# Graph attention on one core: the adjacency cast to bf16 on its way in, by DMAs issued from POOL, two chunks at a time

## The reference

```python
h = jnp.maximum(_layernorm(x, axis=-1), 0.0)          # x: 8 x 2048 x 256 fp32
Wh = jnp.einsum('bnf,fo->bno', h, W)                   # W: 256 x 256
e = (Wh @ a1)[:, :, None] + (Wh @ a2)[:, None, :]
e = jnp.where(e >= 0, e, ALPHA * e)                    # ALPHA = 0.2
attention = jnp.where(adj > 0, e, MASK_FILL)           # adj: 8 x 2048 x 2048 int32
attention = jax.nn.softmax(attention, axis=1)          # over i, the rows
out = x + jax.nn.elu(jnp.einsum('bij,bjo->bio', attention, Wh))
```

## Time and profile before

| | |
|---|---|
| median of 3 runs | 1041.62 us (1041.38 to 1043.15) |
| profiled execution | 1041.01 us |
| its span, first to last instruction | 1039.2 us |
| TensorE busy | 952.9 us, 92% |
| VectorE busy | 962.6 us, 93% |
| ScalarE busy | 937.5 us, 90% |
| POOL busy | 487.7 us, 47% |
| mean granted TensorE clock | 0.994 |
| DMA | 194.82 MB, 323235 packets, 65.6% of 16 engines for the main queue |

### The profile page before, as it was taken

One profiled execution on the slowest core, in us unless ns is written; L12 is line 12 of the kernel. 1 busy time (PEld: TensorE's weight loads), 2 busy tenths in 40 slices (PEclk: granted clock), 3 DMA queues, 4 the chain that ended last, 5 costly groups with the idle time before them and its releaser, 6 DMA issues. The chain is left out here.

```text
span 1039.2 us, 24022 instructions
## 1 busy us (share of the span) xinstructions
PE 952.9 (92%) x8971; PEld 827.7 (80%) x8971; DVE 962.6 (93%) x1259; ACT 937.5 (90%) x1479; POOL 487.7 (47%) x510
## 2 busy tenths in 40 slices
PE   4677999999999999999999999999999999888897
PEld 3565888888888888888888888888888888777786
DVE  5799999999999999999999999999999999999963
ACT  2599999999999999999999999999999999988873
POOL 3344333545445454454545545355454453554543
PEclk9999999999999999999999999999999999999999
DMA  8466565777767677677676767667767666757514
GB/s 233 118 182 185 162 187 162 206 202 203 198 183 208 198 200 212 179 211 201 196 205 178 215 198 204 195 182 207 204 196 208 187 191 175 199 170 200 153 52 152
DMA packets 323235, 194.82 MB, mean 187 GB/s; under 512 B 7472, under 2 KB 319024, under 8 KB 323120
## 3 DMA queue, kind: packets, MB, share of 16 engines
q1 hardware_dynamic: 323120, 193.29, 65.6%
HBM read 176.42 MB, written 16.84 MB: 186 GB/s over the span
## 5 line engine op out<-in xcount | busy, mean ns | idle before, releaser
L418 PE MATMUL acc<-v,direct 128*128 128x256 f16 x1024 | 279.3, 273 | 14.9 <-ACT z_direct L522 7.8
L654 DVE CUSTOM_DVE_ANT_0 prob<-tp,f_row 128x2048 f32<-128x2048 bf16 x128 | 291.8, 2280 | 0.0
L422 PE MATMUL acc<-v,direct 128*128 128x256 f16 x1024 | 279.1, 273 | 0.0
L420 PE MATMUL acc<-v,direct 128*128 128x256 f16 x1024 | 279.1, 273 | 0.0
L401 PE MATMUL acc_st<-v,stored 128*128 128x256 f16 x992 | 270.4, 273 | 0.0
L402 PE MATMUL acc_st<-v,stored 128*128 128x256 f16 x992 | 270.4, 273 | 0.0
L400 PE MATMUL acc_st<-v,stored 128*128 128x256 f16 x992 | 270.4, 273 | 0.0
L743 POOL TENSOR_SCALAR small_total<-total 128x1 f32<-128x1 f32 x128 | 47.7, 373 | 470.4 <-ACT prob L488 470.4
L488 ACT ACTIVATE prob<-prob,shift 128x2048 f32<-128x2048 f32 x128 | 256.5, 2004 | 10.5
L481 ACT ACTIVATE prob<-prob,f 128x2048 f32<-128x2048 f32 x128 | 255.7, 1998 | 0.0
L749 POOL TENSOR_TENSOR direct<-prob,inv 128x1024 f16<-128x1024 f32 x128 | 242.3, 1893 | 10.0
(11 more groups left out here) (81 smaller groups left out, 1263.4 us busy)
## 6 DMA issues: line engine op xcount, KB each, us to landing
raw<-in_adj SPq DMA_DIRECT2D x128, 1024.0 KB, 5.9
y<-in_x SPq DMA_DIRECT2D x64, 256.0 KB, 5.1
out<-y SPq DMA_DIRECT2D x64, 256.0 KB, 3.1
x_in<-in_x SPq DMA_DIRECT2D x108, 128.0 KB, 5.1
f_row<-f_scratch SPq DMA_DIRECT2D x31, 256.0 KB, 5.0
stored<-in_x SPq DMA_DIRECT2D x4, 512.0 KB, 7.8
f_scratch<-f_t SPq DMA_DIRECT2D x124, 0.5 KB
stored<-in_x SPq DMA_DIRECT2D x4, 128.0 KB, 2.2
```

Of the source, the lines that this page charges most:

```text
L418: nc.tensor.matmul(acc[:, m, :], p_d[:, 0, rows], v_c[:, 0, :], start=(j == 0 and m % 2 == 0), stop=False, skip_group_check=True)
L420: nc.tensor.matmul(acc[:, m, :], p_d[:, 0, rows], v_c[:, 1, :], start=False, stop=False, skip_group_check=True)
L422: last = nc.tensor.matmul(acc[:, m, :], p_d[:, 1, rows], v_c[:, 0, :], start=False, stop=(j == C - 1), skip_group_check=True)
L654: nc.vector.tensor_tensor_reduce(out=prob[:, c % 2, :], in0=tp_b, in1=f1_row[:, b % 2, :], scale=1.0, scalar=-3.0e38, op0=ALU.add, op1=ALU ...
```

## The change

The adjacency is brought in as bf16. A DMA that changes the type is issued from POOL, so `load_raw` moves from SP to POOL. It brings two chunks at once: 128 partitions x 16 rows x 256 columns, pieces of 1024 B in memory that become 512 B in `raw`. `raw` keeps two buffers, each now for a pair of chunks in bf16 (the same bytes per buffer as before). Pairs 0 and 1 are issued in steps -17 and -10 ahead of POOL's other work, the others in even steps after the split and the residual addition and before `root`, once the masks of the pair that used the buffer are made. `make_mask` waits on the pair's semaphore and reads its half of the buffer; its operation is the same, with bf16 input in place of int32.

```diff
--- before.py
+++ after.py
@@ -10,7 +10,6 @@
 F32 = mybir.dt.float32
 F16 = mybir.dt.float16
 BF16 = mybir.dt.bfloat16
-I32 = mybir.dt.int32
 
 P = 128
 ALPHA = 0.2
@@ -58,7 +57,7 @@
         def sem(name):
             return ctx.enter_context(nc.semaphore(name))
 
-        raw = sb("raw", [P, 2, C, P], I32)
+        raw = sb("raw", [P, 2, C, 2 * P], BF16)
         neg = sb("neg", [P, 2, C, P], BF16)
         f1_row = sb("f1_row", [P, 2, N], F32)
         prob = sb("prob", [P, 2, N], F32)
@@ -273,11 +272,6 @@
                     sp.wait_ge(xn_ready, c - RX + 1)
                 sp.dma_start(x_buf(c), x[c // C, c % C * P:(c % C + 1) * P, :]).then_inc(x_in_s[(c - EARLY) % RX], 16)
 
-            def load_raw(c):
-                wait(sp, neg_ready, c - 1)
-                sp.dma_start(raw[:, c % 2], adj[c // C].rearrange("(c p) j -> p c j", p=P)[
-                    :, :, c % C * P:(c % C + 1) * P]).then_inc(raw_in[c % 2], 16)
-
             def write_f1(piece):
                 sp.wait_ge(f1_turned, pieces_sent(piece + 1))
                 b, q = divmod(piece, 4)
@@ -303,13 +297,9 @@
                 sp.dma_start(x_early[:, 4 * g:4 * g + 4, :],
                              x[4 * g // C, r:r + 4 * P, :].rearrange("(c p) f -> p c f", p=P)
                              ).then_inc(x_early_in[3 + g], 16)
-            load_raw(0)
-            load_raw(1)
             for c in range(EARLY, EARLY + RX):
                 load_x(c)
             for s in range(FIRST, END + 2):
-                if chunk(s + 3) and s + 3 >= 2:
-                    load_raw(s + 3)
                 if chunk(s + 24) and s + 24 >= EARLY + RX:
                     load_x(s + 24)
                 if chunk(s + LEAD - 1) and (s + LEAD - 1) % 4 == 3 and sent((s + LEAD - 1) // 4):
@@ -637,9 +627,10 @@
                                                op0=ALU.mult, op1=ALU.mult).then_inc(offset_s, 1)
 
             def make_mask(c):
-                dve.wait_ge(raw_in[c % 2], 16 * (c // 2 + 1))
+                pair = c // 2
+                dve.wait_ge(raw_in[pair % 2], 16 * (pair // 2 + 1))
                 wait(dve, tp_ready, c - 1)
-                nc.vector.tensor_scalar(neg[:, c % 2], raw[:, c % 2], 0.0, -NOT_AN_EDGE, ALU.is_le, ALU.mult
+                nc.vector.tensor_scalar(neg[:, c % 2], raw[:, pair % 2, :, c % 2 * P:(c % 2 + 1) * P], 0.0, -NOT_AN_EDGE, ALU.is_le, ALU.mult
                                         ).then_inc(neg_ready, 1)
 
             def mask_scores(c):
@@ -735,6 +726,13 @@
             nc.gpsimd.tensor_copy(ident_b[:], ident[:]).then_inc(ident_ready, 1)
             pool.wait_ge(const_ready, 1)
 
+
+            def load_raw(pair):
+                wait(pool, neg_ready, 2 * pair - 2)
+                b, q = divmod(pair, C // 2)
+                nc.gpsimd.dma_start(raw[:, pair % 2], adj[b].rearrange("(c p) j -> p c j", p=P)[
+                    :, :, 2 * P * q:2 * P * (q + 1)]).then_inc(raw_in[pair % 2], 16)
+
             def split_high(c):
                 p = prob[:, c % 2, :]
                 k = inv[:, c % R:c % R + 1]
@@ -768,10 +766,16 @@
                 nc.gpsimd.tensor_tensor(pair, pair, elu[:, k % RE, :], ALU.add).then_inc(y_ready, 1)
 
             for s in range(FIRST, END + 2):
+                if s == -17:
+                    load_raw(0)
+                if s == -10:
+                    load_raw(1)
                 if chunk(s - 1):
                     split_high(s - 1)
                 for k in finish(s - 2):
                     finish_add(k)
+                if s % 2 == 0 and s >= 0 and chunk(s + 4):
+                    load_raw(s // 2 + 2)
                 if chunk(s + LEAD + 2) and s < 0:
                     normalise(s + LEAD + 2)
                 c = measured_at(s)
```

## The result

The changed kernel takes 1029.26 us (median of 4 runs, 1027.53 to 1030.56); the kernel before, in the same comparison, 1041.84 us (4 runs, 1041.38 to 1043.15). The ratio is 0.9874, 95% interval 0.9861 to 0.9888: 1.3% faster, 12.6 us. Forecast were 1029.0 us. The profiled execution of the changed kernel took 1030.56 us around a span of 1028.8 us, 10.45 us less than that of before.

The account below looks back on a forecast made before the run. VectorE, TensorE and ScalarE, within 2% of each other, form one ring that bounds the kernel. From 1041.0 us, -13.6 - 4.5 + 2 + 3.3 = -12.8 gives 1028.2, as median 1029; own range 1012 to 1037, whole range up to 1085.

Parts of the forecast that it names:

- The mask pass, 0.68 us: VectorE's mask pass: halving the input's bytes halves the time per column again, 1217 ns to 0.68 us, 0.53 us a step.
- What of it reaches the end, 2.0 us a batch: Steps 2 to 110: only what ScalarE gets back of its waits counts, 124.0 in place of 126 us a batch, -13.6 us.
- The steps to show it, 7.75 us: Sign in the steady steps: a step takes 7.75 us, where the profile was read as 7.88.
- The last steps: Last 17 steps, without projection: the mask pass stands once in a ring over two steps, -4.5 us.
- The issue, 2.5 us: POOL's time per new load, taken as 2.5 us between 0.37 and 3.8; in steady steps mostly hidden, +2 us.
- In root steps the root is behind the issue ... VectorE is 0.3 late every fourth step: 0: Steady root steps: root comes 2.2 us later, offsets start 1.85 us after its end; VectorE's 0.53 gain covers it, cost 0.
- Before the first step, +3.3: Start: nothing hides the first two issues among the normalisations; 0.8 us of one and all 2.5 of the other exposed.
- Data and DMA engines, 0: New loads have 16.5 us to land and need 11.8 at the old rate; DMA engines 70% busy: cost 0.
- The issue holds VectorE off: Rival on VectorE: its splits grow past 1.5 us in even steps; chance 0.08.
- POOL becomes the bound: Rival: at an issue of 5 us and more POOL's idle time overflows by 8.4 us a batch, 1089 us; chance 0.22.
- The cast slows the transfer: Rival on the loads: beyond 1.4 times the old time per byte data come late, at 1.6 times about 1160; chance 0.05.
- The pass stays: Rival on the mask pass: it stays at 1.2 us and only the costs are left, 1047 us; chance 0.05.

Follow-up runs that it names:

- the run with the pass alone: The kernel before, its loads unaltered on SP, with the mask pass reading half of each piece as bf16: 1020.62 us, ratio 0.9801.
- the run with the earlier first loads: The changed kernel with `root` ahead of the issue, and the first two loads issued behind the normalisations of steps -19 and -15: 1023.36 us, ratio 0.9833.
- the additions: The changed kernel with `root` ahead of the issue and two small two-input POOL instructions behind each issue from step 0 on: 1049.38 us.

## Why the prediction was right, point by point

- **The mask pass, 0.68 us.** Right: 685 ns, in place of 1217 with four-byte input. Less the 148 ns reckoned as fixed that is 0.26 ns a column, half of 0.52.
- **What of it reaches the end, 2.0 us a batch.** The mechanism was right, the size 16% low: -16.2 us against -13.6 in the run with the pass alone. In the batch from step 64 to 80 ScalarE's idle time falls from 5.3 to 3.2 us there, so the 2.0 were met. The term left out is 0.6 us a batch more, which is not work that went: ScalarE's instructions add up to 133.0 and 132.9 us, but overlap each other by 16.4 us in place of 15.9, as fewer gaps lie between them. The parts of the 2.0 were the wrong way round: it was to be the waits for the projection that go and those for POOL that stay. In that run the projection's stay (1.5 us) and POOL's fall to 0.9. The steps to show it, 7.75 us, came out at 7.48 (814.98 / 109), since they were reckoned from 7.88 in place of 7.64. The last steps: -3.9 and -4.0 against -4.5.
- **The issue, 2.5 us.** No run shows this term. An issue takes 1.25 us (1248 ns, 64 times), half of it, between the price below (0.37) and the lower one above (3.8), nearer to the first.
- **"In root steps the root is behind the issue ... VectorE is 0.3 late every fourth step: 0".** This is the step that failed. It took `root` at its 1.01 us from the earlier trace rows and moved it. Moved behind the issue it starts while VectorE's two-input splits run and takes 1.2 to 2.0, 1.6 on the mean. For three root steps of four the 0 was right all the same. At s = 4 mod 16, where the sum has +0.3 a batch, the addition has pushed it under the second split: VectorE waits 0.93 us for it, and the batch loses 0.84. The route costs 6.3 us in the steady steps where +2 was forecast, in the step that was named, at three times the price; 3.3 of the 6.3 go when `root` stands first. The earlier trace rows has a case of two such instructions side by side, a split of 2.27 us beside an addition of 1.27, where splits with no addition beside them take 1.24 to 1.29; the route's sum holds nothing of the kind for `root`.
- **Before the first step, +3.3.** Measured +3.4 at step 2, of other parts. With the issue at 1.25 us the prediction's own working gives 0 for the first (17.22 is before the 17.71 at which TensorE takes the block) and 1.25 for the second. Of the profiles with these loads in this place and nothing else disturbed, those that keep TensorE's clock have the scores of step 0 at 45.5 us, 1.35 behind the 44.16 with the old loads: the working holds. 1.4 more come in other executions from TensorE's clock (last section), and 1.6 in the profiled one alone, in which the load of the weights landed after 5.1 us (2.9 to 3.5 in the others) and the first normalisation began at 9.32 us (7.1 to 7.7).
- **Data and DMA engines, 0.** Right: no wait of VectorE for a load is listed in the steady stretch, and the issue's wait for the masks is 6.9 us once, early, as the group line shows.

So the total was right in part by luck, since errors cancel: in the steady steps a gain 2.6 us too small and a route cost 4.3 too small, at the start an issue twice too long, which in the executions with a lower clock looks right.

**The rivals.** *The issue holds VectorE off* (chance 0.08), as the addition does with the split in the earlier trace rows (2.27 us): not in the changed kernel. The splits beside issues keep their 1.24 to 1.29 us, and no mask pass lies beside one. Where one does, with `root` first, it goes from 0.68 to 1.38 us (twice), to 1.38 in three steps of the run with the earlier first loads, and to 1.42 in each of six batches with the additions. Once in each of these runs, near 50 us, it was the issue that grew, to 1.62 to 1.63 us, while the pass kept 0.69. So the rival is real for the mask pass and a matter of place: mostly the pass got longer, by 0.70 to 0.74 us, and near 50 us the issue, by 0.4. *POOL becomes the bound:* not at 1.25 us, but nearer than was reckoned. About 4.0 us in place of 1.25 as given make 1091, where the prediction had put the even point at 3.8 us and 1089 only at 5; its count of idle time before the one-column instruction left out that `root` stood behind the issue. 1.86 us still pay (1036.74, two issues per pair); where between that and 4.0 the change stops paying was not measured. *The cast slows the transfer:* not per byte read (63 ns for 1024 B, where two uncast pieces of 512 B take 2 x 34); a pair lands after 9.5 us, where the old rate gave 11.8. *The pass stays:* with a pass of 1386 ns the kernel takes 1054 us; the price of 1047 given for 1217 ns was not tried as such.

Open is what shifts the starts of L621 and of the addition by the few ns that decide between the two patterns at s = 4. In the runs with `root` first, with the earlier first loads, with the pass alone and in the changed kernel, L621 is never held when it starts 3 ns or more ahead (14 of 14) and always when it starts at the same time or later (6 of 6); at 1 to 2 ns ahead it goes either way. The account of the last 2.7 us is read from these traces; no run was made for it. How much of the 42 us between the two orders is the clock's is an estimate from step lengths, not an experiment.

## What to carry to other kernels

An instruction put into a queue costs more than its own length: look at what it pushes back, and at what the pushed instruction will then lie beside. POOL's `root`, with two inputs, took 1.01 us in its old place and 1.96 to 2.15 where it slid under VectorE's two-input work, and VectorE then waited 0.93 us for it. When an engine that feeds others gets a new duty, put the short result that someone waits for ahead of it and the duty last: here that was worth 4 us at 1.25 us of duty and 42 us at 4. Then look again at what the duty lies beside in its new place: here the mask pass, which took 1.38 us in place of 0.68 in two steps.

A pass made 0.53 us shorter, 128 times, gave 20 of 68 us, because two other engines stood within 2% of the bound: read the floors of all engines before the gain is counted.

## What the runs showed of the hardware

- **Issue cost on POOL.** 1.25 us for 2048 pieces, whether these are 1024 B or 512 B in memory (1248 and 1245 ns), 0.93 us for 1024 pieces: here it goes by pieces, with about 0.6 us fixed (an estimate from the two lengths).
- **An issue against a fast VectorE pass.** Beside an issue that started 0.35 us earlier the mask pass (bf16 to bf16, one input) takes 1.38 to 1.42 us in place of 0.68; the two-input fp32 splits beside issues keep their 1.24 to 1.29.
- **A tiny instruction held by a long one.** In the run with `root` first VectorE's one-input L621, 128x4, takes 1.3 us in place of 0.17 when POOL's addition of 1.27 us starts with it.
- **What a casting piece costs the DMA engines.** 0.509 x 1028.8 x 16 / 132096 = 63 ns for 1024 B read and 512 B written; 0.676 x 1028.3 x 16 / 264192 = 42 ns for 512 B read and 256 B written; uncast, 512 B in and out, 0.656 x 1039.2 x 16 / 323235 = 34 ns (that queue holds the other loads too). Casting thus costs 42 ns against 34 for a piece of 512 B, and a piece of 1024 B wins it back: 63 against 2 x 34.
- **Two-byte input with an inner step of 2.** With the columns read and written in two interleaved halves the bf16 pass takes 1386 ns, longer than the int32 one (1217 ns) and twice the 685 ns of the plain one.
- **TensorE's clock after a pause.** The second of the first two issues lengthens TensorE's idle time before the transposes of one block from 1.20 us to 2.42. Two executions have the same program up to step 0 and the same pause, at 30.5 us. In that with `root` first the clock granted over the next microseconds was 0.79, in that with `root` first and two additions it was 1.00 (busy time, 30 to 38 us; the clock is the third number from the end):

```profile
30.00:38.00 8.00, 6.45 (x26) 5.01 (x27) 3.44 (x13) 3.14 (x12) 3.88 (x7) 0.79 1.07 150
```

```profile
30.00:38.00 8.00, 6.21 (x34) 5.08 (x35) 3.41 (x13) 3.64 (x15) 5.37 (x10) 1.00 1.13 158
```

The scores of step 0 start at 46.96 us in the first and at 45.52 in the second, 1.4 apart. In the profiled execution of the changed kernel, after the same 2.42 us, 0.58 was granted from 32 to 36 us, and four projection matmuls took 1.93 us in place of 1.04:

```profile
28.52 1.04 PE L328 MATMUL acc<-w_cat,stored 128*128 128x258 f32 x4
31.98 0.69 PE L340 MATMUL pre<-ident,stored 128*128 128x128 f32 x2 [2.42 <-POOL stored L759]
32.46 1.93 PE L328 MATMUL acc<-w_cat,stored 128*128 128x258 f32 x4
```

So the drop does not follow from the pause each time: of six executions with a pause of 2.42 us three show it, and none of the three with a pause of 1.20 us does. What else decides it stays open.
